# Keys' swapped rotary half made by four ScalarE block copies instead of a second TensorE projection, in a fused decoder layer

## The reference, cut to what matters

```python
def _apply_rotary(pos, t):
    half = t.shape[-1] // 2
    rot = jnp.concatenate([-t[..., half:], t[..., :half]], axis=-1)
    return t * jnp.cos(pos) + rot * jnp.sin(pos)
q = split_heads(_proj(x, Wq, bq))
k = split_heads(_proj(c, Wk, bk))
q = _apply_rotary(q_emb, q)
k = _apply_rotary(k_emb, k)
scores = jnp.einsum('bhtc,bhsc->bhts', q, k) / math.sqrt(K_CH)
```

## Time and profile before, and how to read it

| | us |
|---|---|
| median of three runs | 545.39 |
| the three runs | 547.43, 540.27, 545.39 |
| the profiled execution's own time | 539.41 |
| its span, first to last instruction | 537.3 |

### The profile page before, as it was taken

The page is one execution under the profiler, slowest core; times in us unless marked ns, Lnnn a source line. Parts: engine busy times, 40 slices in busy tenths (PEclk is TensorE's granted clock), DMA queues, the critical chain, the costliest instruction groups (busy, mean ns, idle before and its releaser), DMA issues. The chain is left out here.

```text
span 537.3 us, 11851 instructions
## 1 busy us (share of the span) xinstructions
PE 428.1 (80%) x4098; PEld 231.1 (43%) x4098; DVE 442.1 (82%) x948; ACT 374.3 (70%) x700; POOL 287.1 (53%) x390
## 2 busy tenths in 40 slices
PE   6567799999999999999999999998876602555553
PEld 5354445445454554545545555443332201333332
DVE  3755787989889889799998998988749959999993
ACT  2232266678687786777877867677778778999983
POOL 5841646475474655645557446450124547767653
PEclk9676799999999999999999999999998855555557
DMA  6125326442332322323223232221000000000001
GB/s 226 46 77 182 93 57 187 113 114 69 82 96 63 113 70 67 108 52 111 71 64 112 66 95 69 61 89 42 3 0 1 1 0 1 11 30 20 31 30 40
DMA packets 51674, 37.07 MB, mean 69 GB/s; under 512 B 21408, under 2 KB 47648, under 8 KB 51488
## 3 DMA queue, kind: packets, MB, share of 16 engines
q1 hardware_dynamic: 51328, 36.10, 22.9%
q10 hardware_dynamic: 288, 0.23, 0.2%
HBM read 24.52 MB, written 10.49 MB: 65 GB/s over the span
## 5 line engine op out<-in xcount | busy, mean ns | idle before, releaser
L971 DVE TENSOR_REDUCE MX<-mx_b 128x2 f32<-128x512 f32 x256 | 167.1, 679 | 26.5 <-PE mx_b L581 25.4
L780 ACT ACTIVATE PB<-e_b 128x512 f32<-128x512 f32 x256 | 148.1, 592 | 55.2 <-PE e_b L609 54.0
L581 PE MATMUL mx_b<-KA,QA 48*128 48x256 bf16 x512 | 97.6, 275 | 11.5 <-DVE MX L971 10.8
L609 PE MATMUL e_b<-QA,KA 50*128 50x256 bf16 x512 | 97.1, 274 | 1.0 <-DMA QA<-MR 0.7
L626 PE MATMUL u_b<-PB,VA 128*32 128x256 f32 x1024 | 84.0, 391 | 2.0 <-ACT PB L780 1.5
L898 POOL TENSOR_TENSOR SP<-SP,srec 128x1024 f32<-128x1024 f32 x15 | 28.5, 1901 | 79.1 <-DVE srec L943 79.1
L581 PEld LDWEIGHTS mx_b<-KA,QA 48*128 48x128 bf16 x512 | 29.6, 94 | 86.7 <-issue 47.1
L1301 PE MATMUL r_b<-identh,Q 128*128 128x128 f16 x128 | 16.2, 305 | 39.5 <-ACT Q L1214 39.5
L1246 POOL TENSOR_TENSOR H<-H,row_tab 128x1024 f32<-128x1024 f32 x15 | 35.4, 2363 | 21.4 <-ACT H L1204 17.9
L1307 PE MATMUL z_b<-w2q,Q2T 128*128 128x256 bf16 x128 | 28.5, 400 | 19.3 <-ACT Q2T L1225 19.3
L888 POOL TENSOR_TENSOR KM<-QK,att_tab 128x512 f32<-128x512 f32 x31 | 32.0, 1052 | 21.4 <-ACT QK L734 21.4
(11 more groups left out here) (172 smaller groups left out, 1017.0 us busy)
## 6 DMA issues: line engine op xcount, KB each, us to landing
KA<-parts_k SPq DMA_DIRECT2D x64, 96.0 KB
QA<-parts_q SPq DMA_DIRECT2D x64, 96.0 KB
parts_q<-part_q SPq DMA_DIRECT2D x32, 128.0 KB, 1.9
parts_k<-part_k SPq DMA_DIRECT2D x16, 192.0 KB, 2.1
C<-in_ctx SPq DMA_DIRECT2D x16, 128.0 KB, 3.1
X<-in_x SPq DMA_DIRECT2D x16, 128.0 KB, 2.9
out_y<-O SPq DMA_DIRECT2D x16, 128.0 KB, 1.7
XT<-in_xT SPq DMA_DIRECT2D x15, 128.0 KB, 2.2
```

The lines of the kernel that those rows point to most:

```text
L581: m = nc.tensor.matmul(mx_b[n % 2][:, D * k:D * k + D], QA[low:low + K_MAX, 2 * i.ring + b, h, P * u:P * u + P], KA[low:low + K_MAX, 2 * i ...
L609: m = nc.tensor.matmul(e_b[n % 2][:, D * k:D * k + D], KA[low:low + K_EXP, 2 * i.ring + b, h, P * sc:P * sc + P], QA[low:low + K_EXP, 2 * ...
L780: nc.scalar.activation(PB[:, n % 4].rearrange("p e t -> p (e t)"), e_b[n % 2][:, :], ACT.Exp, scale=XC ** -0.5).then_inc(e_sb.sem, 1)
L971: nc.vector.tensor_reduce(MX[:, b, e, 2 * q:2 * q + 2, u], mx_b[n % 2][:, :].rearrange("p (e s) -> p e s", e=2), AXL.X, ALU.max).then_inc( ...
```

## The change: what it does

The second key projection (L559, weights `kB`) is left out for the 13 pairs a = 3 to 15; the first one moves from step 9 to step 6 of its body. The half-swapped keys are instead made from the first projection: the channels are so laid out that exchanging the halves of a head is exchanging neighbouring blocks of 32 partitions. Four ScalarE copies of 32 partitions by 256 columns take the blocks from bank `g_b[2]` into a new tile `KS`: block 0 after the first half of `self_exp` in step 7, blocks 1 and 2 after the second half, which moves from step 7 to step 8, and block 3 in step 9 behind `mt_copy`. VectorE's sine product reads `KS` instead of the bank, and both of its products now wait for all four copies.

```diff
+        KS = sb("KS", [P, D])
...
+        k_swap = event("k_swap", 4)
...
                 ps = use(bank, ro_sb[n], j, 2)
-                nc.tensor.matmul(ps[:, 0:D], xw[n + "A"], src, start=True, stop=True)
-                nc.tensor.matmul(ps[:, D:2 * D], xw[n + "B"], src, start=True, stop=True).then_inc(ro_ps[n].sem, 1)
+                first = nc.tensor.matmul(ps[:, 0:D], xw[n + "A"], src, start=True, stop=True)
+                if n == "k" and fresh(j):
+                    first.then_inc(ro_ps[n].sem, 1)
+                else:
+                    nc.tensor.matmul(ps[:, D:2 * D], xw[n + "B"], src, start=True, stop=True).then_inc(ro_ps[n].sem, 1)
...
+                    if s == 6 and fresh(a):
+                        rotary_proj("k", g_b[2], a)
                     if s == 7 and real(nxt):
                         xv_proj(nxt)
-                    if s == 9 and fresh(a):
-                        rotary_proj("k", g_b[2], a)
...
+            def exchange_k(j, bank, blocks):
+                wait(act, ro_ps["k"], j, 1)
+                wait(act, ro_sb["k"], j.plus(-1), 2)
+                for k in blocks:
+                    to, at = slice(32 * k, 32 * k + 32), slice(32 * (k ^ 1), 32 * (k ^ 1) + 32)
+                    nc.scalar.activation(KS[to, :], bank[at, 0:D], ACT.Copy).then_inc(k_swap.sem, 1)
...
                     if s == 7 and fresh(a):
                         self_exp(a, 1)
+                        exchange_k(a, g_b[2], (0,))
+                    if s == 8 and fresh(a):
                         self_exp(a, 0)
+                        exchange_k(a, g_b[2], (1, 2))
                     if s == 9 and real(nxt):
                         mt_copy(nxt, 0, 0)
+                    if s == 9 and fresh(a):
+                        exchange_k(a, g_b[2], (3,))
...
+                swapped = n == "k" and fresh(j)
+                if swapped:
+                    dve.wait_ge(k_swap.sem, 4 * (j.v - 2))
                 for m, tab in ((0, cos), (1, sin)):
-                    nc.vector.scalar_tensor_tensor(out=rot[n][:, m, :], in0=bank[:, D * m:D * m + D],
+                    nc.vector.scalar_tensor_tensor(out=rot[n][:, m, :], in0=KS[:] if swapped and m else bank[:, D * m:D * m + D],
```

## The result

The changed kernel takes 574.12 us (median of 4 runs, 570.57 to 577.07), the kernel before in the same comparison 542.83 us. **The ratio is 1.058, 95% interval 1.052 to 1.064: slower by 5.8%.** Forecast were 557.6 us, 2.2%, and a range up to 565. The direction was right; the time is 16.5 us off and outside the range.

What follows compares the result with a forecast made beforehand. TensorE's queue was taken to set body length, except at two waits on other engines. Body 0 0.3, body 1 3.1 and bodies 2 to 12 8.8 made 12.2 us over the median 545.39: 557.6 us, range 548.5 to 565.

Steps and rivals of the forecast that it cites:

- both places: TensorE in steps 6 and 9: waits for `AT` before the projection, making step 7 0.47 us later, and for exp 9 before product 4.
- the first rival: Whole kernel: TensorE's work is what counts, each of 13 pairs 0.43 us shorter, -5.6 us, 539.8 us; chance 0.08.
- Step 6: TensorE: the moved projection waits for `AT`'s copy and begins 0.05 us after it, so step 7 starts 0.47 us later.
- I take 0.27 us in the queue: ScalarE: each copy of 32 partitions by 256 columns was to hold the queue for 0.27 us.
- T+4.29: ScalarE: forecast end of exp 9, in us counted from step 7's start on TensorE, T; product 4 was to come at T+4.33.
- copies and moved exponential: ScalarE work from step 7 on: was to make step 12's transposes 0.33 us late against step 7's start.
- my bounds: ScalarE: a small copy alone lasts 0.28 to 0.38 us; the upper end, 0.38, means no overlap at all in the queue.
- the sum of `SP`: VectorE: starts 0.41 us later against step 7's start and decides the delay, over step 11's tiles at some 0.15 us.
- The sine product: VectorE's rotation: reading `KS` instead of the bank might be a few hundredths shorter, taken as nothing.
- The clock: TensorE falling to 1.2 GHz after body 1's 3.3 us wait: some 3 us, within the dearer-copies-or-more-stalls rival, chance 0.15.
- Body 1: TensorE at step 6 stands still 3.3 us for the late load of `C`, making step 12's transposes 3.1 us later, once.
- "tenths": Projection at step 6: the load of `C` could now and then be late by tenths of a us, body after body.

Runs made afterwards that it cites:

- the filled wait: Changed kernel with the small transposition ahead of product 4 done seven times instead of once, in bodies that have copies; ratio 1.057 to the kernel before, median 569.76 us.

## Why the prediction was wrong, point by point

**Right: the direction and both places.** TensorE waits for `AT` in step 6 and for exp 9 before product 4; the removed matmul time goes there; the first rival (time follows TensorE's work) is dead.

**Step 6, forecast 0.47, is 0.60** (one projection, no copies: 22.51 less 21.91). The projection began 0.14 us after `AT`'s end, not 0.05, and took 0.60 to the product, not 0.53.

**The failed step: "I take 0.27 us in the queue".** A copy that changes rows takes 0.40 us in the queue, and the instruction in front of it 0.13 more than I gave it. So exp 9 ends 0.65 us later than forecast, T+4.94 for T+4.29, and product 4 comes 0.75 later. Forecast for copies and moved exponential were 0.33 us a body; it is 1.00 (23.51 less 22.51). The runs part it:

| part of a body | us | from |
|---|---|---|
| `self_exp(0)` behind exp 8 | 0.10 | 22.01 less 21.91 |
| four copies without change of rows | 0.62 | 23.23 less 22.51 less 0.10 |
| the change of rows | 0.28 | 23.51 less 23.23 |

The first line assumes that the move costs the same in both settings, and the parts overlap. The 0.62 holds the 0.30 us that the transposes wait for the sine product in that kernel; without it the first two lines would be 0.42, near the 0.33 forecast. The 0.28 is what the change of rows adds on top of that wait; on product 4 alone it is the 0.71 us above. It was visible before: the two `VM` copies of the earlier trace rows write rows 0 to 63, then 64 to 127, and start 0.29 apart though the first lasts 0.26, so the second began when the first was done. I halved the 0.56 for a duration and did not ask for the distance. The 0.40 stood outside my bounds, whose dear end, 0.38 a copy, also left the instruction in front at 0.52. There is a second mistake. I let the sum of `SP` decide, because it was the later of two by a little. Moving the exponential alone hardly matters, and in the changed kernel it is exp 9 that decides: each copy in front of it counts in full once the half microsecond between exp 9 and product 4 is spent (211.73 to 212.28).

**The sine product, "taken as nothing".** It is 0.49 us longer, not a few hundredths shorter. That cost 0.05 in the changed kernel, but it is what caps the repairs: without the wait for exp 9 the transposes wait for it.

**The clock, a term put at nothing in the sum and an afterthought in a rival.** I put its fall behind the wait of body 1; it fell behind the wait before product 4, in half of the bodies. It makes 6.4 us in bodies 2 to 11. Body 0 has the same pattern: with and without the filled wait the stretch to the first copy of `AT` differs by 2.65 us, of which 0.38 lie before body 0's copy of `VA`, and body 12 by 1.14. Together about 10 of the 34.9 us. Body 1 is at 0.93 as well; by the other bodies at that clock some 1.2 of its 2.08 us are the clock's, an estimate.

**Body 1, forecast +3.1.** The mechanism was right and hidden: the wait for the context is 1.89 to 3.68 us in all seven kernels whose projection is at step 6 and whose first copy of `AT` starts before 100 us. The "tenths" that I feared in later bodies came as well: in bodies 2 to 12 of five of them the projection waits for `C` here and there, up to 0.93 us where `AT` alone costs 0.48.

**Sum.** 10 x 1.60 + 10.2 for the clock + 2.08 (body 1) + 2.0 (body 12 without its clock share) + 1.2 (body 0 likewise) makes 31.5 of 34.9. The rest is the end of the attention phase and the feed-forward, +3.33, where both kernels do the same work. TensorE's 710 recorded matmuls there take 102.44 us for 99.17, at a mean clock of 0.68 for 0.70; with the wait filled the stretch takes 177.79 us at 0.70, 0.25 more than before. So this too is lower clock; whether the change brings it about is open. Several kernels had bodies of lower clock (down to 0.73) among 12 to 15. Body 12 has a wait of 0.9 to 1.4 us for the rotation in six of them that use `KS`; in bodies 13 to 15 I can name no wait that explains it, so their medians are not to be read as bodies times a period.

No kernel tried beats the one before. The best form of the idea that still computes the rotation, the projection in step 7, is 2.2% slower (1.3 to 3.2%).

## What to carry to other kernels

Time in the queue is not the length of an instruction: read the distance from start to start, for the instruction in front as well, and from a row that moves rows as the new one will. An engine at 70% busy is full in the few steps where others wait for it; put the new work into that stretch before crediting its average slack. And a wait that opens on TensorE can cost twice, once as idle time and again as slower matmuls behind it.

## What the runs showed of the hardware

- **ScalarE between rows.** A Copy of 32 x 256 out of a bank that starts at other rows than its neighbours, in what it reads or in both, starts when they are done (0.65 behind a 0.62 us exponential, 0.40 to the next); in the same rows it is 0.52 and 0.26. The Trainium skill, "VectorE: DVE Perf Modes", section Two Vector instructions with no wait between them, describes for VectorE an instruction that is held until earlier ones have finished when its start quadrant differs from the last one's. The runs show the like on ScalarE, which the page does not speak of.
- **VectorE behind GpSimd.** A product of two SBUF tensors waited until GpSimd's 1.90 us instruction ended and finished 0.28 us later; the time for which it was held lies inside its own duration, 0.97 us. With that instruction at 0.25 us it took 0.48. The product that reads a bank never waited. The Trainium skill, "SBUF — State Buffer", section SBUF: two separate sides, says that such an operation and a GpSimd operation that reads SBUF exclude each other for a whole instruction, the one that starts first going first. The trace agrees.
- **TensorE's clock.** Behind waits of 1.31 to 1.32 us before product 4 the granted clock fell to 1.2 GHz in about half of the bodies and not in the others; in the kernels whose wait there was 1.12 us or less, or filled, and whose waits in step 12 were 0.58 us or less, bodies 2 to 11 all stayed at 1.00. The two with the copies in step 9, which wait 0.71 us and then 0.84 or 1.20 us in step 12, had bodies at 0.93 and, once, 0.87. What tells the two halves apart is open; it is not chance alone, since in all six profiles with such bodies 7 and 8 are among the slower and 9 is not.
